# An adapter on 128 batches: order of the first weight piece's work, and who adds a bias at the end

## The reference

```
h = gelu(x @ W_down[role] + b_down[role])       # 1024 -> 512, exact gelu
y = x + h @ W_up[role] + b_up[role]             # 512 -> 1024
out = (y - mean(y)) / sqrt(var(y) + 1e-5) * gamma[role] + beta[role]
```

## Time and profile before

| | |
|---|---|
| median of 3 runs | 1424.69 us (1423.2 to 1425.12) |
| profiled execution | 1424.26 us, span 1422.4 us |
| TensorE (PE) busy | 1405.7 us, 99% |
| VectorE (DVE) busy | 1203.8 us, 85% |
| ScalarE (ACT) busy | 782.5 us, 55% |
| GpSimd (POOL) busy | 195.1 us, 14% |
| DMA | 283.52 MB, mean 199 GB/s over the span |

### The profile page before, as it was taken

How to read it: one execution, slowest core, us unless ns; L and a number is a source line. 1 busy time by engine, 2 the same in 40 slices (tenths; PEclk the granted TensorE clock), 3 DMA queues, 4 the chain that set the end, 5 groups by cost and what they waited for, 6 DMA issues and landing times.

```text
span 1422.4 us, 32330 instructions
## 1 busy us (share of the span) xinstructions
PE 1405.7 (99%) x6175; PEld 1156.3 (81%) x6176; DVE 1203.8 (85%) x1454; ACT 782.5 (55%) x2059; POOL 195.1 (14%) x297
## 2 busy tenths in 40 slices
PE   8999999999999999999999999999999999999997
PEld 6888888888888888888888888888888888888885
DVE  7798988888888888888888899888888888888888
ACT  5555555555555555555555555555555555555555
POOL 3376411100000000000000377310100000000000
PEclk9999999999999999999999999999999999999999
DMA  9688777766666666666666778776776666667663
GB/s 222 177 232 229 217 211 205 199 199 205 185 190 197 196 182 196 196 197 183 188 204 192 209 230 225 222 201 193 204 217 186 197 203 185 184 194 203 187 193 139
DMA packets 208726, 283.52 MB, mean 199 GB/s; under 512 B 25775, under 2 KB 155312, under 8 KB 208702
## 3 DMA queue, kind: packets, MB, share of 16 engines
q1 hardware_dynamic: 201726, 269.60, 63.5%
q0 software_dynamic: 5888, 12.07, 5.1%
q10 hardware_dynamic: 1088, 1.57, 0.4%
HBM read 183.27 MB, written 99.88 MB: 199 GB/s over the span
## 4 chain that ended last, share of the span: by engine, by line
PE 96%; DVE 1%; DMA 1%; issue 1%; ACT 1%; SPq 0%; DVEq 0%
PE p_down L989 16%; PE p_down L990 16%; PE p_down L991 16%; PE p_up L989 16%; PE p_up L990 16%; PE p_up L991 16%; DMA row<-in_L_cond_W_down 0%; DVEq L241 0%; SPq L267 0%; SPq L258 0%; DMA h_quad<-h_dram 0%; DMA h_dram<-h 0%; DVE row L805 0%; PE p_hT L985 0%; DVE x_quad L921 0%
## 5 line engine op out<-in xcount | busy, mean ns | idle before, releaser
L989 PE MATMUL p_down<-wd_hi,xT_hi 128*128 x1012 | 395.4, 391 | 0.2
L991 PE MATMUL p_down<-wd_hi,xT_lo 128*128 x1012 | 393.9, 389 | 0.0
L990 PE MATMUL p_down<-wd_lo,xT_hi 128*128 x1012 | 393.9, 389 | 0.0
L989 PE MATMUL p_up<-wu_hi,hT_hi 128*128 x1008 | 392.7, 390 | 0.1
L991 PE MATMUL p_up<-wu_hi,hT_lo 128*128 x1008 | 392.3, 389 | 0.0
L990 PE MATMUL p_up<-wu_lo,hT_hi 128*128 x1008 | 392.3, 389 | 0.0
L559 ACT ACTIVATE hT_hi<-p_hT 128x512 fp32r<-128x512 f32 x126 | 75.5, 599 | 435.4 <-DVE p_hT L724 432.6
L744 DVE SCALAR_TENSOR_TENSOR row<-p_up,row 128x1024 f32<-128x1024 f32 x126 | 154.2, 1224 | 170.8 <-PE p_up L991 135.1
L989 PEld LDWEIGHTS p_down<-wd_hi,xT_hi 128*128 128x128 f32 x1012 | 189.9, 188 | 45.0 <-issue 5.2
L989 PEld LDWEIGHTS p_up<-wu_hi,hT_hi 128*128 128x128 f32 x1008 | 189.2, 188 | 42.0 <-issue 1.6
L991 PEld LDWEIGHTS p_down<-wd_hi,xT_lo 128*128 128x128 f32 x1012 | 190.0, 188 | 39.9
(11 more groups left out here) (164 smaller groups left out, 955.6 us busy)
## 6 DMA issues: line engine op xcount, KB each, us to landing
x_quad<-in_x SPq DMA_DIRECT2D x510, 128.0 KB, 3.6
row<-in_x SPq DMA_DIRECT2D x126, 512.0 KB, 4.1
out<-row SPq DMA_DIRECT2D x126, 512.0 KB, 2.8
h_dram<-h SPq DMA_DIRECT2D x125, 256.0 KB, 4.3
h_quad<-h_dram SPq DMA_DIRECT2D x500, 64.0 KB, 2.0
w_raw<-in_L_cond_W_down POOLq DMA_DIRECT2D x64, 64.0 KB, 3.7
w_raw<-in_L_cond_W_up POOLq DMA_DIRECT2D x64, 64.0 KB, 3.8
row<-in_L_cond_W_up SPq DMA_DIRECT2D x16, 128.0 KB, 5.8
```

The source lines that it names most:

```text
L989: pe.matmul(dst, a_hi, w_hi, start=first, stop=False)
L990: pe.matmul(dst, a_hi, w_lo, start=False, stop=False)
L991: return pe.matmul(dst, a_lo, w_hi, start=False, stop=last)
```

## The change

In the head: two of the four transfers of piece 2 are issued by ACT ahead of its wait for the first batch numbers, no longer behind the rounding of piece 0. The lo of piece 1 is made in two halves of 512 columns, one ahead of the subtraction for half 0 of batch 0 and one behind it, and TensorE waits for each by itself. The transpose of half 1 of batch 0 moves from ahead of that subtraction to behind the transpose of half 0 of batch 1; the subtractions for (batch 1, half 0) and (batch 0, half 1) change places, and ACT's roundings likewise. TensorE runs two matmuls on a buffer that GpSimd has set to zero, right after the matmul that orders the batches; of the four fillers after the spreads it runs one, then one more once the first half of x is rounded. In the tail: GpSimd adds the up bias to x of batches 126 and 127 at the end of its program, after a wait for x and for up products (a counter that is 2 after batch 0 and one more for each batch); VectorE's two adds and one lookup go; the output of batch 124 is written in step 128 ahead of the subtraction of h of batch 127, not behind it.

```diff
 # gpsimd
             pool.memset(opener[:, 0:2], 0.0).then_inc(pieces_split, 1)
+            pool.memset(xT_lo[:, 0:HALF, :].bitcast(F32), 0.0).then_inc(zeros_ready, 1)
...
                 load_params(r, params_at, part)
 
+            for b in range(B - 2, B):
+                at = entry_value(PARAMS_AT * B + b, PARAMS)
+                pool.wait_ge(up_bias_loaded, 16 * R)
+                pool.wait_ge(quad_loaded[b % 2], 16 * NQ * (B // 2) + 16)
+                pool.wait_ge(up_done, b - 1)
+                pool.tensor_tensor(row_of(b, 0), row_of(b, 0), cols(params, at + BU, H), ALU.add).then_inc(last_plus_bias, 1)
 # scalar
             load_first(act, 0, range(1, NQ))
             load_first(act, 1)
+            load_first(act, FD - 2, range(0, NQ // 2))
             act.wait_ge(first_known, 1)
             load_quads(act, act.value_load(first_numbers[0:1, 0:1], min_val=0, max_val=B - 1), 0, range(NQ // 2, NQ))
...
             round_first(0)
-            load_first(act, FD - 2, range(0, NQ // 2))
             act.wait_ge(order_in_psum, 1)
...
             round_first(1)
             round_half(0, 0)
-            round_half(0, 1)
             copy_param(2, p_up[1][:, :], BETA, H, beta_loaded)
             copy_param(1, p_hT[:, :], BD, K, bias_loaded)
             round_half(1, 0)
+            round_half(0, 1)
             round_first(2)
 # vector
+            def split_chunk(n, c, done):
+                buf, hi, lo, _ = first_piece(n)
+                at = slice(c * K, c * K + K)
+                dve.wait_ge(first_hi, n + 1)
+                dve.tensor_tensor(lo[:, at], buf[:, at], hi[:, at].bitcast(F32), ALU.subtract).then_inc(done, 1)
...
             def subtract_half(b, half):
                 hi, lo = half_x(b, half)
+                if (b, half) == (0, 0):
+                    dve.wait_ge(zeros_used, 1)
...
             def sum_y(b, par, ring):
                 y = row_of(b, ring)
                 dve.wait_ge(up_done, b + 2)
-                dve.wait_ge(x_plus_bias, b + 2 if isinstance(b, int) and b == B - 3 else b + 1)
+                if isinstance(b, int) and b >= B - 2:
+                    dve.wait_ge(last_plus_bias, b - B + 3)
+                else:
+                    dve.wait_ge(x_plus_bias, b + 1)
...
             def body(i, k):
...
-                for d in (-4, -3, -2, -1, 0):
+                for d in (-4, -3, -2, 0):
...
                 if live(seq(i, k, 1)[0]):
                     transpose_x(*seq(i, k, 1))
 
+                if is_step(i, k, B):
+                    write_out(i, k, at)
+
                 b = turned(i, k)
                 if live(b):
                     subtract_h(b)
 
+                if not is_step(i, k, B):
+                    write_out(i, k, at)
...
-                    if is_last(b):
-                        add_bias(b - 1, 0, 0, at[-1])
                     bias_h(b, at[0], p_down[:, :])
...
-                if is_step(i, k, B - 1):
-                    add_bias(B - 1, 0, 0, at[0])
...
             split_first(0)
             transpose_half(0, 0)
-            transpose_half(0, 1)
+            split_chunk(1, 0, chunk_split)
             subtract_half(0, 0)
-            split_first(1)
+            split_chunk(1, 1, first_split)
...
             transpose_half(1, 0)
+            transpose_half(0, 1)
+            subtract_half(1, 0)
             subtract_half(0, 1)
-            subtract_half(1, 0)
             transpose_half(1, 1)
 # tensor
+            pe.wait_ge(zeros_ready, 1)
+            for _ in range(2):
+                mm = pe.matmul(p_down[:, :], xT_lo[:, 0, :], xT_lo[:, 0:HALF, :], start=True, stop=True)
+            mm.then_inc(zeros_used, 1)
             pe.wait_ge(first_hi, 1)
             keep_clock(2)
...
-            keep_clock(4)
+            keep_clock(1)
+            pe.wait_ge(half_hi, 1)
+            keep_clock(1)
...
             def half_product(b, half, dst, at):
                 hi, lo = half_x(b, half)
                 for c in range(half * HALF, half * HALF + HALF):
-                    if b == 0 and c % (FC // K) == 0:
+                    if (b, c) == (0, FC // K):
+                        pe.wait_ge(chunk_split, 1)
+                    elif (b, c) == (0, FC // K + 1):
+                        pe.wait_ge(first_split, 2)
+                    elif b == 0 and c % (FC // K) == 0:
                         pe.wait_ge(first_split, c // (FC // K) + 1)
```

More of the change, by code:

```diff
@@ L143, in adapter_kernel @@
         param_rows_clear, row_known = sem("param_rows_clear"), sem("row_known")
+        zeros_ready, zeros_used, chunk_split = sem("zeros_ready"), sem("zeros_used"), sem("chunk_split")
         ident_ready, params_spread, params_landed = sem("ident_ready"), sem("params_spread"), sem("params_landed")
@@ L162, in adapter_kernel @@
         last_half_up, last_step, last_out = sem("last_half_up"), sem("last_step"), sem("last_out")
-        last_std_ready = sem("last_std_ready")
+        last_std_ready, last_plus_bias = sem("last_std_ready"), sem("last_plus_bias")
         half_var_ready = sem("half_var_ready")
@@ L732, in add_bias @@
             def add_bias(b, ring16, ring, at):
[L733 to L736, removed]
+                dve.wait_ge(row_loaded[ring], ring16 + 16)
                 dve.tensor_tensor(row_of(b, ring), row_of(b, ring), cols(params, at + BU, H),
@@ L769, in scale_y, with write_out @@
                                          ALU.mult).then_inc(scaled, 1)
+            def write_out(i, k, at):
+                b, _, par = seq(i, k, -4)
+                if live(b):
+                    y = row_of(b, turn(i, k, -4)[1])
+                    if not late(b, 4):
+                        dve.wait_ge(beta_loaded, look_up(dve, WHEN_LOADED, b, 16, 16 * R))
+                    dve.wait_ge(scaled, b + 1)
+                    dve.wait_ge(rstd_ready[NEWTON], b + 1)
+                    dve.scalar_tensor_tensor(y, y, rstd[NEWTON][:, par:par + 1],
+                                             cols(params, at[-4] + BETA, H), ALU.mult, ALU.add).then_inc(out_ready, 1)
             def body(i, k):
                 at = {}
-                for d in (-4, -3, -2, -1, 0):
+                for d in (-4, -3, -2, 0):
                     b = seq(i, k, d)[0]
-                    if live(b) and (d != -1 or is_step(i, k, B - 1)):
+                    if live(b):
                         at[d] = look_up(dve, PARAMS_AT, b, 0, PARAMS)
@@ L901, in _ @@
             y = row_of(b, ring)
-            dve.wait_ge(x_plus_bias, b + 1)
+            dve.wait_ge(last_plus_bias, 2)
             dve.wait_ge(last_half_up, 1)
```

## The result

The changed kernel takes 1428.36 us (median of 9 runs, 1427.07 to 1430.38) against 1424.95 beside it before: a ratio of 1.0028, interval 1.0019 to 1.0036, so **slower by about 3.4 us**. I had forecast 1424.6 and no change. The profiled execution takes 1427.14 us with a span of 1425.3, against 1424.26 and 1422.4.

What follows compares the result with a forecast made beforehand. TensorE, busy 99% of the span, was taken as the bound, leaving only head and tail open. Head -0.2 and tail +0.1 gave -0.1 us on 1424.26, an execution 0.43 under the median: forecast 1424.6, range 1423.0 to 1426.2.

Steps and rivals of the forecast that it cites:

- Head, TensorE: cost nothing, as long as its clock is up: Head, TensorE: first product at about 13.3 in place of 13.03, staying 0.2 to 0.5 us under VectorE's path, costing nothing.
- x of batch 0: Head, DMAs: last quarter of the first x lands at 11.0, bounds 10.3 and 11.3, up to 0.94 us later.
- the idle stretch: Head, DMAs: engines 63% busy from 6.0 to 7.6; filling this hole is worth 0.6 us of traffic to everything behind.
- The second x: Head, DMAs: x of batch 1 should land at about 13.5 in place of 14.0.
- Rival C: Head: x0 lands at 11.5 or later behind W_down, VectorE's row starts after 14.2; +0.3 and +0.1, 1425.1; chance 0.15.
- Tail: Tail: GpSimd's add delays VectorE's output step of batch 123 and the last bias add; +0.1 us, bounds -0.55 and +0.4.
- rival A: Tail gains in full, GpSimd's add and output step missing each other: -0.2 - 0.55 = -0.75 us, 1423.9; chance 0.27.
- Rival B: Head: TensorE's clock rises later, slow first product; up to +1.9 us, 1426.6; chance 0.13, beyond 2.85 us 0.03.
- my 13.5: Head, TensorE: the granted clock rises at 13.5, 0.2 us after the first product's start, so hidden.

Runs made afterwards that it cites:

- old_fillers: The changed kernel with the four fillers of before in a row and no wait between them; 2.35 us under the changed kernel.
- wait_only: The kernel before with its four fillers replaced by one, the wait for the first rounded half of x, and one; median +1.18 us against before.
- fill_order: old_fillers with VectorE's transpose of half 1 of batch 0 moved right behind the subtraction for half 0; median 0.02 us above before.
- w_early_only: The kernel before with only the two W_down issues moved ahead; median -0.78 us against before, interval with zero.
- tail_only: The head of before with the changed tail; +0.63 us against before, interval with zero.
- pool_late: The changed kernel with GpSimd's add for batch 127 waiting until VectorE has written batch 123; median 1.6 us under the changed kernel.
- head_only: The changed head with the tail of before; +2.94 us against before.
- early_lookups: The changed kernel with TensorE's three slot lookups ahead of its wait for the first rounded half of x; +1.8 us against before, changed kernel +3.4.
- fill_w_late: old_fillers with the two W_down issues back behind the rounding of piece 0; medians differ by 0.26 us only, ratios not at all.
- best: Head order of before with early W_down issue and two zero matmuls, changed tail with GpSimd's add behind VectorE's output of batch 123; no faster than before.

## Why the prediction was wrong

**The step that failed** is "Head, TensorE: cost nothing, as long as its clock is up". I counted the two fillers that the change saves and not what stands in the queue behind the wait that it adds. The lookups are what TensorE's program does next behind the last filler and one more wait, and the kernel before shows them at 8.7 to 10.8, under the spreads. They start after the wait: 2.1 us, of which 0.7 lies beside the last filler and the operand's arrival, the rest ahead of the first product (15.58 in place of my 13.3). The condition failed too: behind the pause, four executions of five ran their products at the 1.2 GHz pace. The runs give 2.4 us of the 3.4 to this wait with its fillers (old_fillers), and +1.2 to it alone (wait_only). How much is the pause and how much the clock stays open.

**A second step left out**: I moved `transpose_half(0, 1)` on VectorE's queue and asked only who waits for it on ACT. SP waits for it too, before its loads of the third x. Price in the changed kernel nothing, as TensorE is later still; 0.7 to 1.0 us as soon as the first cost is gone (fill_order against old_fillers).

**x of batch 0** landed at 7.06 + 4.6 = 11.6; I took 11.0 between 10.3 and 11.3. The two transfers did use the idle stretch (DMA share 0.99 from 6 to 8 us in place of 0.71), but the latency of x grew from 4.2 to 4.6, and its issue came 0.95 later. The second x came at 8.7 + 5.4 = 14.1, no earlier than before, so the hole of 0.6 us that I counted as a gain for everything behind was worth nothing to it. Rival C was right about the place and, by w_early_only, the median does not show its price.

**Tail.** The mechanism was right to the row: GpSimd's add 2.40 (I took 2.6), the output step behind it 2.85, ending 1.08 after it. The term was mis-sized: +0.1 against a measured +0.6 (tail_only). The landing took 5.6 us in place of 4.7, so the add began 0.63 ahead of the output step and not 0.75 to 0.85 ahead, and the bias add came 0.48 later, and the sum of batch 126 another 0.5: VectorE's three lookups ahead of it took 2.3 (1409.1 to 1411.4) in place of 1.8 (1406.7 to 1408.5), which I had not priced. Without the collision the tail's mark stands at 26.3 in the mean of six executions, against 26.7 in the mean of the four with the tail of before (26.3 to 27.0): about -0.4, not the 0.55 of rival A.
The Trainium skill, "SBUF — State Buffer", "Who interferes with whom", has two such instructions exclude one another for a whole instruction. The trace agrees once more: 1396.08 + 2.40 + 1.08 gives the end of the output step, and pool_late shows the step at 1.28 without the add beside it.

**Rival B** named TensorE's clock and the size of the outcome (up to +1.9 and beyond), by a late rise, and I gave it 0.13, and 0.03 to a result over 0.2%. head_only and early_lookups show such a late rise, at 21.9 and 17.8 in place of my 13.5. The second and third executions and pool_late show what I had not thought of: a clock that was up and was lost around a 2 us pause of the kernel's own making. I gave the rival too small a chance, and its cause covers two of the five traces at half pace.

## What to carry to other kernels

A wait that is put into an engine's program delays everything behind it on that queue, register lookups first of all: three of them are 2.1 us here, free under queued matmuls and bare behind a wait. Put lookups ahead of waits. Look also at the pace behind such a pause: in four executions of five the products there ran at half pace for some 3 us or more, in three of them after the clock had been up. A moved instruction has readers on other engines than the one the move was made for; list every semaphore that it raises and every queue that waits on it. When work goes from VectorE to GpSimd, look at which two-input instruction of VectorE it will meet at the moment its data lands; one wait that puts it behind that instruction was worth about 1 us of the tail.

## What the runs showed of the hardware that was not expected

- The granted clock fell to half around a pause of 2.0 us that followed nearly unbroken work since 6.6, in the second and third executions of the changed kernel and in pool_late: 16.1 to 19.4, 15.2 to 18.6, 15.9 to 19.4. In the first execution the same program ran fast behind the pause.
- The fillers of these three executions of one program turned fast at different moments: by 12.0 in the third, near 12.8 in the second, and in the first not before 13.8. The Trainium skill, "TensorE: Matmul & The Clock Gate", Part 1, has the moment of the rise differ between executions of one kernel. The three executions agree.
- Two kernels with two fillers in place of four came to the fast pace only at 17.8 (early_lookups, no pause) and 21.9 (head_only, with the pause); wait_only, with two as well, near 12.5. The kernels with four came to it between 10.5 (fill_w_late) and 15 (best), before at 12.5. One execution each, so this is no rule.
- TensorE's stretch between the marks, the same work in all, took 1351.3 to 1354.0 us. The scatter of 2 to 3 us among a kernel's runs is mostly there, and no experiment under 1 us is settled by one execution.
